# Attention stage of a two-block image kernel: scores, maxima and exponentials by pairs of head quads, values as 64-column halves, another order

## The chip, the cores and the metric

The kernel runs on one core of one Trainium2 chip. Its time is the device time of one execution in microseconds; lower is better. A core has five engines that each take their own instructions in order: PE (matrix products), DVE (vector), ACT (scalar, activations), POOL, and SP, which here issues the transfers. They wait for one another by semaphores.

## The reference, cut to what matters

The input `x` is (4, 128, 112, 112). Two blocks follow each other, each a residual on a group norm of its input. The change touches the first alone, attention in windows of 8x8 pixels with 8 heads of 16:

```
win = windows of gn(x), 64 tokens each           # 14 x 14 windows an image
xn  = layernorm(win) * ln_gamma + ln_beta
q, k, v = split(xn @ w_qkv.T + b_qkv)            # 8 heads, d = 16
scores  = einsum('nhqd,nhkd->nhqk', q * d**-0.5, k)
o   = einsum('nhqk,nhkd->nhqd', softmax(scores), v)
x   = x + (o @ w_out.T + b_out)                  # back from windows to image
x   = x + block_2(gn(x))                         # linear attention, 3x3 conv, MLP of 1024
```

## The kernel before, in words

Three stages follow each other: the window attention (lines 1367 to 1428 for PE), the contexts of the second block (`strip_c`), and its MLP (`step_d`). Only the first is changed.

An image has 14 strips of 8 rows, a strip 14 windows. A strip is worked on as two groups: `gg = 0` has 4 pairs of windows (512 tokens), `gg = 1` has 3 (384). `G` counts the groups over all images, 112 of them. `group_loop` (L306) calls each engine's `step(G, ...)` for each group; the strips in the middle of an image run in a hardware loop, the others are written out. Each `step` is a list in a fixed order, and each engine goes through its own: the order of the calls in the source is the order of the queue. A step mixes work on groups G-2 to G+3.

The work on a group, in the order of its data: ACT normalises the image strip into `xg` (`gn_apply`); PE transposes it to tokens in bank 5 (`ln_transpose`); DVE takes statistics (`ln_stats`, `ln_moments`), POOL the reciprocal root (`ln_rstd`), DVE writes `xc` (`ln_norm`); PE transposes back (`ln_back`), ACT writes `xn` and its high part (`xn_evac`), POOL its low part (`xn_low`). PE projects q (bank 7), k (bank 4) and v (bank 7): `project_q`, `project_k` by three split products each, `project_v` by one matmul for each pair of windows. ACT writes `qs` and two masked copies of k (`kx`), POOL casts both to bf16 (`q16`, `k16`), DVE copies v into `vx` in four pieces (`v_evac`, `value_blocks`).

The 8 heads lie as four quads `j` of 32 rows (two heads each). `score_rows` writes bf16 scores of quad j, queries in rows, to bank j; DVE takes their row maxima (`maxima`); PE transposes these (`transpose_maxima`, to bank 6) and DVE copies them (`mt_evac`). `score_cols` writes into the same banks j minus the maximum (L1334) and adds the fp32 scores with keys in rows (L1339); ACT takes exponentials into the one buffer `prob` (`exps`), and PE must not write the next score rows before (`prob_ready`). `attend` multiplies `prob` with `vx`, whose ones columns give the sums, half `h = 1` of a group (its last windows) into bank 7, half 0 into bank 6; DVE divides (`normalise`). `out_transpose` and `out_project` (bank 4), `ot_evac`, `ob_evac`, and POOL's `residual` add it to the image. DVE also takes the statistics for the group norms: of the next image (`next_stats`) and of the finished strip (`strip_stats`).

PE's `step` is, in order: score_rows(G), out_transpose(G-2), attend(G-1, 1), ln_transpose(G+2), out_project(G-2), attend(G-1, 0), transpose_maxima(G), project_q and project_k(G+1), score_cols(G), project_v(G+1), ln_back(G+2). DVE's: maxima(G), normalise(G-1, 1), ln_stats(G+2), mt_evac(G), ln_moments(G+2), normalise(G-1, 0), strip_stats (gg = 1), ln_norm(G+2), v_evac(G+1), next_stats (gg = 0).

Of the kernel before, what the change touches and what calls it, by code (L numbers as in the profile page):

```python
# [30 lines left out]
P = 128  # L31
# [46 lines left out]
def build(nc, x_d, vec_d, fc1b_d, dw_d, wm_d, cm_d, w1_d, w2_d, sel_d, out_d):  # L78
    with ExitStack() as ctx:
# [25 lines left out]
        qb = sb("qb", [P, NIMG])  # L105
        pws = [sb(f"pw_{n}", [P, 2, P], F32R) for n in ("hi", "lo")]
# [52 lines left out]
        prob = sb("prob", [P, QUADS, 8, 64], F32, stack_b)  # L159
# [12 lines left out]
        tstl = sb("tstl", [P, 2, STRIP], F32R, stack_b)  # L172
        kv = sb("kv", [P, 2, 4, 2, 2, P], F32, stack_b)
# [64 lines left out]
        smax_mm = sem("smax_mm")  # L238
# [3 lines left out]
        st_mm = sem("st_mm")  # L242
        prob_ready = sem("prob_ready")
# [135 lines left out]
        def value_blocks(gg):  # L379


            n = GROUP_PAIRS[gg]
            for w2 in range(2):
                for s in range(2):
                    src = bank[7][64 * w2:64 * w2 + 64, 0:P * n]\
                        .rearrange("p (t j s d) -> p t j s d", j=QUADS, s=2, d=HD)[:, :, :, s, :]
                    yield vx[64 * s:64 * s + 64, gg, w2:2 * n:2, :, (HD + 1) * s:(HD + 1) * s + HD], src
# [107 lines left out]
        def _(pool):  # L495
# [53 lines left out]
            def prologue():  # L549
                ln_rstd(0, 0)  # L550
                xn_low(0, 0)
                ln_rstd(1, 1)
                cast_q(0, 0)
                cast_k(0, 0)
# [7 lines left out]
            def step(G, i, s, gg, near):  # L562
                ng = 1 - gg
                if near(1):
                    xn_low(G + 1, ng)
                if near(-2):
                    residual(G - 2, strip_back(i, s)[1], gg)
                if near(2):
                    ln_rstd(G + 2, gg)
                if near(1):  # L570
                    cast_q(G + 1, ng)
                    cast_k(G + 1, ng)
                if at_norms(i, s) and gg == 0:
                    gn_coef(i + 1, norms_at(i))
# [45 lines left out]
        def _(act):  # L620
# [48 lines left out]
            def exps(G, gg):  # L669

                n = P * GROUP_PAIRS[gg]
                act.wait_ge(st_mm, G + 1)
                for j in range(QUADS):
                    m = a.activation(prob[:, j, 0:n // 64].rearrange("p w q -> p (w q)"), bank[j][:, 0:n], ACT.Exp)  # L674
                m.then_inc(prob_ready, 1)

            def ot_evac(G, gg):


                n = P * GROUP_PAIRS[gg]  # L680
                act.wait_ge(ot_mm, G + 1)
                a.activation(ot[:, gg, 0:n], bank[4][:, 0:n], ACT.Identity, bias=v("bv")).then_inc(ot_ready, 1)
# [7 lines left out]
            def prologue():  # L690
                act.wait_ge(gcoef_ready, 1)
                gn_apply(0, 0, 0, 0)
                gn_apply(1, 0, 0, 1)
                xn_evac(0, 0)
                gn_apply(2, 0, 1, 0)
                q_evac(0, 0)
                k_evac(0, 0)
                xn_evac(1, 1)

            def step(G, i, s, gg, near):  # L700
                ng = 1 - gg
                if near(-2):
                    ot_evac(G - 2, gg)
                    ob_evac(G - 2, gg)
                if near(3):
                    if at_norms(i, s) and gg == 1:
                        act.wait_ge(gcoef_ready, i + 2)
                    gn_apply(G + 3, *strip_after(i, s, 1 + gg), ng)
                if near(1):
                    q_evac(G + 1, ng)  # L710
                    k_evac(G + 1, ng)
                exps(G, gg)
# [115 lines left out]
        def _(dve):  # L828
# [45 lines left out]
            dve.wait_ge(weights_hi, 1)  # L874
            d.tensor_tensor(pws[1][:], wm[:, 0:2, :], pws[0][:].bitcast(F32), ALU.subtract).then_inc(weights_lo, 1)
# [87 lines left out]
            def maxima(G, gg):  # L963
                n = GROUP_PAIRS[gg]
                dve.wait_ge(smax_mm, G + 1)
                for j in range(QUADS):
                    m = d.tensor_reduce(mx[:, gg, 32 * j:32 * j + 2 * n],  # L967
                                        bank[j][:, 0:P * n].rearrange("p (e k) -> p e k", k=64), AX.X, ALU.max)
                m.then_inc(max_ready, 1)

            def mt_evac(G, gg):
                dve.wait_ge(mt_mm, G + 1)
                d.tensor_copy(mt16[:, gg, :], bank[6][:, 448:512].bitcast(BF16)).then_inc(mt_ready, 1)
# [49 lines left out]
            def prologue():  # L1023
                ln_stats(0, 0)
                ln_moments(0, 0)
                ln_norm(0, 0)
                ln_stats(1, 1)
                ln_moments(1, 1)
                ln_norm(1, 1)
                v_evac(0, 0)  # L1030

            def step(G, i, s, gg, near):
# [13 lines left out]
                mt_evac(G, gg)  # L1046
                if norms:
                    norm_variance(i + 1, norms_at(i), 6)
                if i + 1 < NIMG and isinstance(s, int) and s == 0:
                    next_stats(i, gg)  # L1050
                if near(2):
                    ln_moments(G + 2, gg)
                if near(-1):
                    normalise(G - 1, ng, 0)
                if gg == 1 and near(-2):
                    strip_stats(*strip_back(i, s), G - 1)
                if near(2):
                    ln_norm(G + 2, gg)
                if near(1):
                    v_evac(G + 1, ng)  # L1060
# [187 lines left out]
        def _(pe):  # L1248
# [50 lines left out]
            def project_v(G, gg):  # L1299
                for t in range(GROUP_PAIRS[gg]):  # L1300
                    c = slice(P * t, P * t + P)
                    m = mm(bank[7][:, c], xn[:, gg, c], wmat("wv"), start=True, stop=True)  # L1302
                m.then_inc(v_mm, 1)
# [5 lines left out]
            def score_rows(G, gg, reuse):  # L1309
# [4 lines left out]
                if reuse:  # L1314
                    pe.wait_ge(prob_ready, G)
                for w in range(2 * GROUP_PAIRS[gg]):
                    t, w2 = w // 2, w % 2
                    for j in range(QUADS):
                        m = mm(bank[j][64 * w2:64 * w2 + 64, P * t:P * t + P], q16[quad_rows(j), gg, w, :],  # L1319
                               k16[quad_rows(j), gg, w, :, :].rearrange("p s k -> p (s k)"), start=True, stop=True)  # L1320
                m.then_inc(smax_mm, 1)

            def transpose_maxima(G, gg):
                pe.wait_ge(max_ready, G + 1)
                tr(bank[6][:, 448:512].bitcast(BF16), mx[:, gg, :], ident16[:]).then_inc(mt_mm, 1)

            def score_cols(G, gg):
# [4 lines left out]
                for t in range(GROUP_PAIRS[gg]):  # L1332
                    for j in range(QUADS):
                        mm(bank[j][:, P * t:P * t + P], sel16[quad_rows(j), t, :], mt16[quad_rows(j), gg, :],  # L1334
                           start=(t == 0), stop=True, skip_group_check=True)
                for w in range(2 * GROUP_PAIRS[gg]):
                    for s in range(2):
                        for j in range(QUADS):
                            m = mm(bank[j][64 * s:64 * s + 64, 64 * w:64 * w + 64], kx[quad_rows(j), gg, w, s, :],  # L1339
                                   qs[quad_rows(j), gg, w, :], start=False, stop=True, skip_group_check=True)  # L1340
                m.then_inc(st_mm, 1)

            def attend(G, gg, h):


                for t in range(2 * h, min(2 * h + 2, GROUP_PAIRS[gg])):
                    for j in range(QUADS):
                        for q in range(4):
                            c, w = (t % 2) * QUADS * VCOLS + j * VCOLS, 2 * t + q // 2
                            m = mm(bank[6 + h][32 * q:32 * q + 32, c:c + VCOLS],  # L1350
                                   prob[:, j, w, 32 * (q % 2):32 * (q % 2) + 32], vx[:, gg, w, j, :],
# [3 lines left out]
            def out_transpose(G, gg):  # L1355
                pe.wait_ge(oh_ready[0], G + 1)
                pe.wait_ge(oh_ready[1], G + 1)
                for t in range(GROUP_PAIRS[gg]):
                    m = tr(bank[4][:, P * t:P * t + P], oh[:, gg, P * t:P * t + P], cmat("ident"))
# [7 lines left out]
            def prologue():  # L1367
# [4 lines left out]
                pe.wait_ge(xnl_ready, 1)  # L1372
                project_q(0, 0)
                project_k(0, 0)
                pe.wait_ge(q_ready, 1)
# [3 lines left out]
            def step(G, i, s, gg, near):  # L1379
                ng = 1 - gg  # L1380
                norms = at_norms(i, s) and gg == 0
                score_rows(G, gg, near(-1))
                if near(-2):
                    out_transpose(G - 2, gg)
                pe.wait_ge(v_ready, G + 1)
                if near(-1):
                    attend(G - 1, ng, 1)
                if near(2):
                    pe.wait_ge(xn_ready, G + 2)
                    ln_transpose(G + 2, gg)  # L1390
                if near(-2):
                    out_project(G - 2, gg)
                if near(-1):
# [4 lines left out]
                transpose_maxima(G, gg)  # L1398
                if near(1):
                    pe.wait_ge(xnl_ready, G + 2)  # L1400
                    if near(-1):
# [12 lines left out]
            def epilogue():  # L1414
                pe.wait_ge(ob_ready, NG - 2)
                out_transpose(NG - 2, 0)
                pe.wait_ge(prob_ready, NG)
                pe.wait_ge(v_ready, NG)
                attend(NG - 1, 1, 1)
                out_project(NG - 2, 0)  # L1420
                attend(NG - 1, 1, 0)
                pe.wait_ge(ob_ready, NG - 1)
                out_transpose(NG - 1, 1)
# [231 lines left out]
```

## Time and profile before

| | us |
|---|---|
| time, median of 3 runs (2667.43 to 2674.15) | 2669.88 |
| the profiled execution | 2671.07 |
| its span, first to last instruction | 2669.1 |
| busy PE | 2468.9 (92%) |
| busy DVE | 2159.1 (81%) |
| busy ACT | 2157.9 (81%) |
| busy POOL | 1716.4 (64%) |

The profile page gives these sums, the busy share of each engine over time, the chain of work that ended last, and the costliest groups of instructions. Rows of the trace name an instruction by its line in the kernel before. An engine can be said to wait for an instruction of another: "idle before, <-releaser". A matmul of fp32 operands appears as two instructions. Durations hold the time until the result is written, so the rows of an engine with a full queue overlap.

### The profile page before, as it was taken

What the parts mean: (1) busy time and instruction counts of PE and PEld (TensorE: products, weight loads), DVE (VectorE), ACT (ScalarE), POOL (GpSimd) and SP (SyncE); (2) the same over time, 40 slices, a digit from 0 to 9 for tenths busy, and PEclk for the clock granted to TensorE, in tenths of its full rate; (3) what the DMA queues carried; (4) which work ended last, traced back from release to release, by engine and by line L of the source; (5) the groups of instructions that cost most, each with busy time, mean ns of one, the idle gap of its engine ahead of it and who ended that gap; (6) DMA issues with size and microseconds to landing.
All of it is one profiled execution on the core that took longest, in us unless ns stands there. A gap on an engine that the chain in (4) does not pass through costs nothing.

```text
span 2669.1 us, 107195 instructions
## 1 busy us (share of the span) xinstructions
PE 2468.9 (92%) x43420; PEld 2088.9 (78%) x43420; DVE 2159.1 (81%) x4875; ACT 2157.9 (81%) x4093; POOL 1716.4 (64%) x1714
## 2 busy tenths in 40 slices
PE   3888789888888899899989999999999999999999
PEld 2666566666666667688978988898898899889888
DVE  6888788888988888667788888888888888888885
ACT  2777567766777777566779999999999999999998
POOL 2555445544555455366647777777777777777778
PEclk9999899999999999899989999999999999999999
DMA  4222122212221111144401101111110111100000
GB/s 151 70 76 72 51 82 76 75 59 78 78 74 53 48 55 49 50 136 127 138 15 42 41 32 42 42 42 38 42 42 32 42 41 42 39 28 21 17 21 25
DMA packets 55794, 152.18 MB, mean 57 GB/s; under 512 B 6608, under 2 KB 20944, under 8 KB 55632
## 3 DMA queue, kind: packets, MB, share of 16 engines
q1 hardware_dynamic: 55632, 149.93, 17.3%
q8 instruction: 113, 1.85, 0.3%
q14 instruction: 49, 0.40, 0.0%
HBM read 98.52 MB, written 51.38 MB: 56 GB/s over the span
## 4 chain that ended last, share of the span: by engine, by line
PE 72%; DVE 18%; issue 4%; ACT 2%; POOL 2%; DVEq 0%; SPq 0%; DMA 0%; POOLq 0%; ACTq 0%
PE bank L1285 17%; PE bank L1287 17%; PE bank L1286 17%; DVE mx L967 7%; PE bank L1440 6%; PE bank L1339 4%; DVE vx L960 3%; PE bank L1507 3%; PE bank L1302 2%; ACT prob L674 2%; DVE gst L835 2%; PE bank L1350 1%; DVE xc L953 1%; PE bank L1453 1%; POOL lnrs L526 1%
## 5 line engine op out<-in xcount | busy, mean ns | idle before, releaser
L613 POOL TENSOR_TENSOR hl<-hf,hh 128x448 fp32r<-128x448 f32 x896 | 1025.2, 1155 | 307.5 <-ACT hf L796 301.3
L795 ACT ACTIVATE hh<-bank,fc1i 128x448 fp32r<-128x448 f32 x896 | 584.9, 653 | 67.1 <-PE bank L1287 61.4
L1168 DVE SCALAR_TENSOR_TENSOR bank<-oring,dw,bank 128x448 f32<-128x448 f32 x896 | 614.9, 686 | 20.0
L796 ACT ACTIVATE hf<-bank,fc1i 128x448 f32<-128x448 f32 x896 | 586.2, 654 | 0.0
L1285 PE MATMUL bank<-t1h,w_hi 128*128 128x448 f32 x896 | 365.6, 408 | 5.9 <-DVE t1l L1187 5.6
L1285 PE MATMUL bank<-hh,w_hi 128*128 128x448 f32 x896 | 328.2, 366 | 0.0
L1287 PE MATMUL bank<-hl,w_hi 128*128 128x448 f32 x896 | 327.9, 366 | 0.0
L1287 PE MATMUL bank<-t1l,w_hi 128*128 128x448 f32 x896 | 327.4, 365 | 0.0
L1286 PE MATMUL bank<-hh,w_lo 128*128 128x448 f32 x896 | 327.2, 365 | 0.0
L1286 PE MATMUL bank<-t1h,w_lo 128*128 128x448 f32 x896 | 326.6, 365 | 0.0
L532 POOL TENSOR_TENSOR xn_lo<-xn,xn_hi 128x512 fp32r<-128x512 f32 x112 | 128.7, 1149 | 252.0 <-ACT xn_hi L651 252.0
L967 DVE TENSOR_REDUCE mx<-bank 128x8 bf16<-128x512 f32 x448 | 248.2, 616 | 11.1 <-PE bank L1319 8.2
L674 ACT ACTIVATE prob<-bank 128x512 f32<-128x512 f32 x448 | 207.4, 549 | 53.3 <-PE bank L1339 52.7
L560 POOL TENSOR_TENSOR ximg<-ximg,ob 128x512 f32 (+1 forms) x112 | 127.6, 1139 | 180.9 <-ACT ob L687 180.9
L960 DVE COPY vx<-bank 64x256 f32<-64x256 f32 x448 | 174.2, 389 | 62.5 <-PE bank L1302 57.9
L1350 PEld LDWEIGHTS bank<-vx,prob 128*32 128x32 f32 x12544 | 132.5, 110 | 110.2 <-issue 91.8
L1285 PEld LDWEIGHTS bank<-t1h,w_hi 128*128 128x128 f32 x896 | 168.7, 188 | 39.7 <-issue 26.7
L1286 PEld LDWEIGHTS bank<-t1h,w_lo 128*128 128x128 f32 x896 | 168.7, 188 | 32.3 <-issue 20.4
L1173 DVE TENSOR_TENSOR dwl<-bank,dwh 128x448 fp32r<-128x448 f32 x112 | 69.9, 624 | 144.2 <-ACT dwh L782 144.2
L953 DVE TENSOR_SCALAR xc<-bank,lnmv,lnrs 128x128 f32<-128x128 f32 x392 | 134.3, 402 | 58.6 <-POOL lnrs L526 58.6
L1287 PEld LDWEIGHTS bank<-hl,w_hi 128*128 128x128 f32 x896 | 168.3, 188 | 14.3
L687 ACT ACTIVATE ob<-bank,vec 128x512 f32<-128x512 f32 x112 | 71.0, 634 | 134.1 <-PE bank L1365 134.1
(167 smaller groups left out, 5966.4 us busy)
## 6 DMA issues: line engine op xcount, KB each, us to landing
ximg<-x SPq DMA_DIRECT2D x112, 448.0 KB, 3.4
ximg<-x_in SPq DMA_DIRECT2D x56, 448.0 KB, 3.4
x<-ximg SPq DMA_DIRECT2D x56, 448.0 KB, 2.5
y_out<-yb SPq DMA_DIRECT2D x112, 224.0 KB, 1.9
xs<-x_in SPq DMA_DIRECT2D x42, 448.0 KB, 3.4
wm<-wm_in SPq DMA_DIRECT2D x1, 512.0 KB, 5.3
w1f<-w_in SPq DMA_DIRECT2D x1, 512.0 KB, 8.8
w<-w_in SPq DMA_DIRECT2D x1, 512.0 KB, 9.6
```

What stands on the lines that cost most here:

```text
L613: g.tensor_tensor(hl[:, k, :], hf[:, k, :], hh[:, k, :].bitcast(F32), ALU.subtract).then_inc(hl_ready, 1)
L674: m = a.activation(prob[:, j, 0:n // 64].rearrange("p w q -> p (w q)"), bank[j][:, 0:n], ACT.Exp)
L795: a.activation(hh[:, j, :], p, ACT.Gelu, bias=bias)
L796: a.activation(hf[:, j, :], p, ACT.Gelu, bias=bias).then_inc(hf_ready, 1)
L953: m = d.tensor_scalar(xc[:, gg, P * t:P * t + P], bank[5][:, P * t:P * t + P], lnmv[:, gg, t, 0:1], lnrs[:, gg, t:t + 1], ALU.subtract, AL ...
L960: m = d.tensor_copy(dst, src)
L967: m = d.tensor_reduce(mx[:, gg, 32 * j:32 * j + 2 * n], bank[j][:, 0:P * n].rearrange("p (e k) -> p e k", k=64), AX.X, ALU.max)
L1168: m = d.scalar_tensor_tensor(acc, src, dw[:, k:k + 1], acc, ALU.mult, ALU.add)
L1285: mm(out, w[0], x[0], start=start, stop=False)
L1286: mm(out, w[1], x[0], start=False, stop=False)
L1287: return mm(out, w[0], x[1], start=False, stop=stop)
L1440: m = mm(bank[2 + cc][:, 2 * P * t:2 * P * t + 2 * P], x[:, sp, c], w.rearrange("p a b -> p (a b)"), start=(k == 0), stop=(k == 2))
```

## The change

- Scores, maxima and exponentials are done by pairs of quads: half `h` is quads 2h and 2h+1, with semaphores of its own (`smax_mm`, `st_mm`, `prob_ready`). `prob` has two buffers, by `gg`.
- `project_v` makes, for each window, two matmuls of 64 columns, for the first and the second head of all quads (`wvs` holds the weights so sorted), into the lower and upper 64 partitions of bank 4. `v_evac` copies each half by one instruction of 64 partitions, two for four.
- Banks: v goes from 7 to 4, the transposed maxima from 6 to 7, `out_transpose` from 4 to 6.
- Orders of all four engines' steps change. On PE `transpose_maxima` stands before `attend(G-1, 0)`, `project_k` comes before and `project_q` between the two halves of `score_cols` (half 1 first). On DVE both `normalise` follow `ln_moments`, then come the first half of `v_evac(G+1)`, `ln_norm`, `strip_stats` and the second half of `v_evac`.

```
+            for w in range(2 * GROUP_PAIRS[gg]):
+                for e in range(2):
+                    m = mm(bank[4][64 * e:64 * e + 64, 64 * w:64 * w + 64], xn[:, gg, 64 * w:64 * w + 64],
+                           wvs[:, e, :], start=True, stop=True)
             m.then_inc(v_mm, 1)
...
-            def v_evac(G, gg):
+            def v_evac(G, gg, e):
+                n = GROUP_PAIRS[gg]
                 dve.wait_ge(v_mm, G + 1)
-                for dst, src in value_blocks(gg):
-                    m = d.tensor_copy(dst, src)
-                m.then_inc(v_ready, 1)
+                src = bank[4][64 * e:64 * e + 64, 0:P * n].rearrange("p (w j d) -> p w j d", j=QUADS, d=HD)
+                d.tensor_copy(vx[64 * e:64 * e + 64, gg, 0:2 * n, :, (HD + 1) * e:(HD + 1) * e + HD], src)\
+                    .then_inc(v_ready, 1)
...
DVE step:
-                maxima(G, gg)
-                if near(-1):
-                    normalise(G - 1, ng, 1)
+                for h in range(2):
+                    maxima(G, gg, h)
                 if near(2):
                     ln_stats(G + 2, gg)
+                mt_evac(G, gg)
...
                 if near(2):
                     ln_moments(G + 2, gg)
...
                 if near(-1):
+                    normalise(G - 1, ng, 1)
                     normalise(G - 1, ng, 0)
+                if near(1):
+                    v_evac(G + 1, ng, 0)
+                if near(2):
+                    ln_norm(G + 2, gg)
                 if gg == 1 and near(-2):
                     strip_stats(*strip_back(i, s), G - 1)
-                if near(2):
-                    ln_norm(G + 2, gg)
                 if near(1):
-                    v_evac(G + 1, ng)
+                    v_evac(G + 1, ng, 1)
...
PE step:
-                score_rows(G, gg, near(-1))
+                if gg == 0:
+                    score_rows(G, gg, 0, near(-1))
                 if near(-2):
                     out_transpose(G - 2, gg)
-                pe.wait_ge(v_ready, G + 1)
+                if gg == 1:
+                    score_rows(G, gg, 0, near(-1))
+                score_rows(G, gg, 1, near(-1))
                 if near(-1):
                     attend(G - 1, ng, 1)
                 if near(2):
                     pe.wait_ge(xn_ready, G + 2)
                     ln_transpose(G + 2, gg)
+                pe.wait_ge(v_ready, G * 2 + 2)
                 if near(-2):
                     out_project(G - 2, gg)
+                transpose_maxima(G, gg)
                 if near(-1):
                     attend(G - 1, ng, 0)
...
-                transpose_maxima(G, gg)
                 if near(1):
                     pe.wait_ge(xnl_ready, G + 2)
+                    if near(-2):
+                        pe.wait_ge(ob_ready, G - 1)
+                    project_k(G + 1, ng)
+                score_cols(G, gg, 1)
+                if near(1):
                     if near(-1):
                         pe.wait_ge(oh_ready[1], G)
                     project_q(G + 1, ng)
-                    if near(-2):
-                        pe.wait_ge(ob_ready, G - 1)
-                    project_k(G + 1, ng)
-                score_cols(G, gg)
+                score_cols(G, gg, 0)
                 if near(1):
-                    pe.wait_ge(q_ready, G + 2)
+                    pe.wait_ge(k_ready, G + 2)
                     project_v(G + 1, ng)
                 if near(2):
                     ln_back(G + 2, gg)
```

On ACT the step becomes ot_evac, gn_apply, ob_evac, k_evac, exps half 1, q_evac, exps half 0, xn_evac (before: ot_evac, ob_evac, gn_apply, q_evac, k_evac, exps, xn_evac). On POOL `ln_rstd` goes ahead of `residual` and `cast_k` ahead of `cast_q`.

## Rows read from the trace of the kernel before

**Rows 1.** The page, chain that ended last, share of the span by engine.

```profile
PE 72%; DVE 18%; issue 4%; ACT 2%; POOL 2%; DVEq 0%; SPq 0%; DMA 0%; POOLq 0%; ACTq 0%
```

**Rows 2.** Windows, one strip: busy PE, PEld, DVE, ACT, POOL (instructions), clock, DMA, GB/s.

```profile
658.40:676.88 18.48, 16.53 (x585) 12.47 (x585) 16.56 (x51) 13.78 (x25) 9.81 (x13) 1.00 0.22 74
```

**Rows 3.** Waits from 300 to 1100 us: total us, times, longest.

```profile
PE bank L1319 <- ACT prob L674: 42.2, 82, 1.0
...
DVE vx L960 <- PE bank L1302: 41.1, 51, 2.6
```

**Rows 4.** Timeline of DVE: start, us, engine, line, op, xcount [idle before].

```profile
658.40 2.48 DVE L967 TENSOR_REDUCE mx<-bank 128x8 bf16<-128x512 f32 x4
660.80 0.20 DVE L980 RECIPROCAL rden<-bank 128x8 f32<-128x8 f32 x1
...
664.23 1.37 DVE L953 TENSOR_SCALAR xc<-bank,lnmv,lnrs 128x128 f32<-128x128 f32 x4 [0.98 <-POOL lnrs L526]
665.51 1.46 DVE L960 COPY vx<-bank 64x192 f32<-64x192 f32 x4
667.00 1.15 DVE L835 BATCH_NORM_STATS2 gst<-xs 128x448 f32 x2
668.19 1.95 DVE L967 TENSOR_REDUCE mx<-bank 128x6 bf16<-128x384 f32 x4
...
675.12 1.73 DVE L960 COPY vx<-bank 64x256 f32<-64x256 f32 x4 [0.57 <-PE bank L1302]
676.88 2.49 DVE L967 TENSOR_REDUCE mx<-bank 128x8 bf16<-128x512 f32 x4
```

**Rows 5.** Timeline of DVE in the last image, two strips' first maxima.

```profile
995.45 2.48 DVE L967 TENSOR_REDUCE mx<-bank 128x8 bf16<-128x512 f32 x4
...
1013.21 2.48 DVE L967 TENSOR_REDUCE mx<-bank 128x8 bf16<-128x512 f32 x4
```

**Rows 6.** Timelines of PE, and of ACT for the exponentials, in the same strip.

```profile
660.26 0.77 PE L1350 MATMUL bank<-vx,prob 128*32 128x34 f32 x64
660.96 0.23 PE L1325 MATMUL bank<-ident,mx 128*128 128x128 bf16 x1
...
662.68 0.40 PE L1334 MATMUL bank<-mt,sel 32*128 32x128 bf16 x16
663.01 1.59 PE L1339 MATMUL bank<-qs,kx 32*64 32x64 f32 x128
664.53 0.94 PE L1302 MATMUL bank<-wm,xn 128*128 128x128 f32 x6
665.65 0.65 PE L1280 MATMUL bank<-cm,xc 128*128 128x128 f32 x4 [0.18 <-DVE xc L953]
...
672.46 0.35 PE L1334 MATMUL bank<-mt,sel 32*128 32x128 bf16 x12
...
673.92 1.16 PE L1302 MATMUL bank<-wm,xn 128*128 128x128 f32 x8
...
664.64 2.06 ACT L674 ACTIVATE prob<-bank 128x512 f32<-128x512 f32 x4 [0.62 <-PE bank L1339]
```

**Rows 7.** The chain of waits from 658 to 677 us: start, us, what.

```profile
672.08 0.23 PE bank L1286
```

**Rows 8.** PE's timeline at idle stretches, and windows: granted clock third from last.

```profile
600.68 0.23 PE L1325 MATMUL bank<-ident,mx 128*128 128x128 bf16 x1 [2.14 <-DVE mx L967]
...
830.67 0.59 PE L1268 MATMUL bank<-gdev,cm 128*128 128x2 f32 x2 [3.00 <-DVE gdev L925]
...
871.24 0.23 PE L1325 MATMUL bank<-ident,mx 128*128 128x128 bf16 x1 [1.58 <-DVE mx L967]
...
1123.76 1.11 PE L1359 MATMUL bank<-cm,oh 128*128 128x128 f32 x4
...
828.40:835.10 6.70, 4.43 (x104) 3.80 (x109) 4.62 (x22) 1.81 (x3) 2.40 (x5) 0.59 0.01 2
```

More of the change, by code:

```diff
@@ L105, in build @@
         qb = sb("qb", [P, NIMG])
+        wvs = sb("wvs", [P, 2, P // 2])
         pws = [sb(f"pw_{n}", [P, 2, P], F32R) for n in ("hi", "lo")]
@@ L172, in build @@
         tstl = sb("tstl", [P, 2, STRIP], F32R, stack_b)
+        stack_p = ExitStack()
+        prob = sb("prob", [P, 2, QUADS, 8, 64], F32, stack_p)
+        stack_p.close()
         kv = sb("kv", [P, 2, 4, 2, 2, P], F32, stack_b)
@@ L237, in build @@
         k16_ready = sem("k16_ready")
-        smax_mm = sem("smax_mm")
+        smax_mm = [sem(f"smax_mm{n}") for n in range(2)]
         max_ready = sem("max_ready")
@@ L241, in build @@
         mt_ready = sem("mt_ready")
-        st_mm = sem("st_mm")
-        prob_ready = sem("prob_ready")
+        st_mm = [sem(f"st_mm{n}") for n in range(2)]
+        prob_ready = [sem(f"prob_ready{n}") for n in range(2)]
         pv_mm = sem("pv_mm")
@@ L377, in ring_copies, with quad_pair @@
                    ([(0, BLOCK_ROWS - 1)] if u == 3 and after else [])
[L379 to L387, printed above, removed]
+        def quad_pair(h):
+            return range(2 * h, 2 * h + 2)
         def hold(eng):
@@ L667, in k_evac, with exps @@
                              scale=v("mask_hi")).then_inc(k_ready, 1)
-            def exps(G, gg):
+            def exps(G, gg, h):
                 n = P * GROUP_PAIRS[gg]
[L672 to L675, printed above, removed]
+                act.wait_ge(st_mm[h], G + 1)
+                for j in quad_pair(h):
+                    m = a.activation(prob[:, gg, j, 0:n // 64].rearrange("p w q -> p (w q)"), bank[j][:, 0:n], ACT.Exp)
+                m.then_inc(prob_ready[h], 1)
             def ot_evac(G, gg):
@@ L874, in _ @@
             dve.wait_ge(weights_hi, 1)
+            d.tensor_copy(wvs[:].rearrange("p e (j d) -> p e j d", j=QUADS),
+                          wmat("wv").rearrange("p (j e d) -> p e j d", j=QUADS, e=2))
             d.tensor_tensor(pws[1][:], wm[:, 0:2, :], pws[0][:].bitcast(F32), ALU.subtract).then_inc(weights_lo, 1)
@@ L955, in ln_norm, with maxima @@
                 m.then_inc(xc_ready, 1)
-            def v_evac(G, gg):
+            def v_evac(G, gg, e):
+                n = GROUP_PAIRS[gg]
                 dve.wait_ge(v_mm, G + 1)
-                for dst, src in value_blocks(gg):
-                    m = d.tensor_copy(dst, src)
-                m.then_inc(v_ready, 1)
-            def maxima(G, gg):
+                src = bank[4][64 * e:64 * e + 64, 0:P * n].rearrange("p (w j d) -> p w j d", j=QUADS, d=HD)
+                d.tensor_copy(vx[64 * e:64 * e + 64, gg, 0:2 * n, :, (HD + 1) * e:(HD + 1) * e + HD], src)\
+                    .then_inc(v_ready, 1)
+            def maxima(G, gg, h):
                 n = GROUP_PAIRS[gg]
-                dve.wait_ge(smax_mm, G + 1)
-                for j in range(QUADS):
+                dve.wait_ge(smax_mm[h], G + 1)
+                for j in quad_pair(h):
                     m = d.tensor_reduce(mx[:, gg, 32 * j:32 * j + 2 * n],
@@ L1029, in prologue @@
                 ln_norm(1, 1)
-                v_evac(0, 0)
+                v_evac(0, 0, 0)
+                v_evac(0, 0, 1)
             def step(G, i, s, gg, near):
@@ L1337, in score_cols @@
                     for s in range(2):
-                        for j in range(QUADS):
+                        for j in quad_pair(h):
                             m = mm(bank[j][64 * s:64 * s + 64, 64 * w:64 * w + 64], kx[quad_rows(j), gg, w, s, :],
                                    qs[quad_rows(j), gg, w, :], start=False, stop=True, skip_group_check=True)
-                m.then_inc(st_mm, 1)
+                m.then_inc(st_mm[h], 1)
             def attend(G, gg, h):
@@ L1372, in prologue @@
                 pe.wait_ge(xnl_ready, 1)
+                project_k(0, 0)
                 project_q(0, 0)
-                project_k(0, 0)
-                pe.wait_ge(q_ready, 1)
+                pe.wait_ge(k_ready, 1)
                 project_v(0, 0)
@@ L1414, in epilogue @@
             def epilogue():
-                pe.wait_ge(ob_ready, NG - 2)
                 out_transpose(NG - 2, 0)
-                pe.wait_ge(prob_ready, NG)
-                pe.wait_ge(v_ready, NG)
+                for h in range(2):
+                    pe.wait_ge(prob_ready[h], NG)
+                pe.wait_ge(v_ready, NG * 2)
                 attend(NG - 1, 1, 1)
```

54 lines of the change are left out of this document (26 added, 28 removed).

## The prediction

> **What bounds the kernel now.** I read the page's share of the chain first, then the windows, then the waits, then one undisturbed strip engine by engine. The chain over the whole run is PE for 72% [rows 1], but most of that is the last stage, which the change leaves alone. The attention stage is the stretch from 48 to about 1128 us, 56 strips of two groups (4 and 3 window pairs). There no engine is at its limit: in one strip PE is busy 16.53 of 18.48 us and DVE 16.56 [rows 2]. The waits of the stage show who ends them: DVE for the value projection 51 times, by 41 us in all, PE for the exponentials 82 times, by half a microsecond each [rows 3]; both are short. The DVE rows of a strip are nearly without a hole: 0.98 us before `xc`, 0.57 us before `vx`, and the next strip begins 18.48 us after the last [rows 4]. So the stage is DVE's queue, with a little of PE's in it. A loop through both engines runs close under it: maxima end, PE projects, computes the score columns and the values, DVE copies the values, maxima begin again. In the strip of rows 4 it ended the wait for `vx` by 0.57 us. The last image has no statistics of a next image, and its strip takes 17.76 us [rows 5].
>
> I take occupancies from start to next start, since queued instructions overlap in the rows.
>
> **What changes on DVE.** The value copy becomes 2 instructions of 64x512 (or 384) for 4 of 64x256 (192). 4 of 256 take 1.76 us (675.12 to 676.88), 4 of 192 1.49 us (665.51 to 667.00) [rows 4]: 0.44 and 0.37 each, so 1.06 ns per column and 0.17 us fixed; 512 columns make 0.70 us and 384 0.57. That is 2.54 us a strip for 3.25: 0.7 us of DVE work goes. From below, at the rate of the maxima of the same width (0.60 and 0.47), it is 2.14. If DVE stayed the bound this would be the gain. Two probability buffers and halves with their own semaphores also let score rows of one pair of quads begin before the other pair's exponentials are done. But PE waits only that 0.5 us a group for the exponentials [rows 3], and DVE's order, not these waits, decides when maxima start. I count it nothing; it is worth at most 0.5 a group.
>
> **The new order makes the loop longer on both engines.** All engines take their instructions in order, so I walk the loop once per group, from M (maxima done) to P (`project_v` done) on PE and from P to the next M on DVE.
>
> From M to P, for both groups of a strip:
> - The maxima transpose and its handover, 0.2 each: 0.40. It starts about 0.1 us after the maxima end [rows 4, 6].
> - `attend(G-1, 0)`, which now stands behind the transpose that waits for the maxima, where before it ran beside them: 64 instructions in 0.70 us (660.26 to 660.96) [rows 6], twice 0.70: 1.40. This was hidden and is now on the path.
> - `project_k` and `project_q`, 3 matmuls each of 0.23 for 512 columns [rows 7] and three quarters of it for 384: 0.70 + 0.52 for each of the two: 2.44, as before.
> - The score columns. Now they take 1.85 (662.68 to 664.53) and 1.46 (672.46 to 673.92): 3.31 [rows 6]. In halves, two quads' row groups are at work instead of four. L1334 takes 0.33 for 16 and 0.28 for 12, 0.055 a round of four over a fixed 0.1; a half still needs a round per pair of windows, so it costs what the whole does: up to 0.61 more. L1339 runs at 11.9 ns over eight tiles (1.52 us for 128). One stream of 64 columns is half of the 0.11 us of a 128-column transpose, so with four tiles no better than 13.8 ns: 0.4 more, and a new start in each half. From below nothing is lost; from above each L1339 takes the 20.6 ns that L1334 has with four tiles, 2.5 us more in all. I take 0.9, nearest to the rounds: 4.21.
> - `project_v`: in place of 4 matmuls of 128 columns (0.99 us) and 3 (0.77) come 16 and 12 of 64 columns, each two instructions, 32 and 24, in two column tiles of the array. If the two overlap, 0.0275 each (1.54 us together), if they don't, 0.055 (3.1). Rows with four column tiles and all 128 rows (L1350) run at 11 ns for 34 columns, so they overlap, not fully: I take 0.0345, 1.93.
> - The handover to DVE, 0.2 each: 0.40.
>
> The sum is 10.8 us a strip. DVE has, after M, only the layer-norm statistics, the maxima copy, moments and both normalisations. The same instructions stand between the maxima and the wait for the roots now, from 660.80 to 663.25 (664.23 less 0.98) [rows 4]: 2.5 us a group. Then `v_evac(G+1, 0)` heads its queue and waits for P, about 5.4 us after M. That is the new stall, 2.5 to 3 us a group.
>
> From P to M on DVE, both groups:
> - both value copies of each group, 2.54.
> - `ln_norm`, now behind the first of them: 1.28 (664.23 to 665.51) for four, three quarters of it and a little for three, 1.00: 2.28. It used to run while PE was still at the score columns.
> - `strip_stats` in the one group (now behind the copy too) and `next_stats` in the other (as before), 667.00 to 668.19 less a wait's turn, 1.13 each: 2.26.
> - the maxima, 2.40 (658.40 to 660.80) + 1.87: 4.27.
>
> Sum 11.35. The other queues are not late: on ACT the last two exponentials start with the end of the columns and take 1.0 us (four take 2.06 [rows 6]), so they are done about when P is and before `ln_back`; the k copies run beside the first half of the columns; POOL is busy 9.81 of 18.48 us [rows 2], and `mt_ready` comes at M + 1.1 us, before PE reaches the first half at M + 1.5. SP's transfers keep their places by strip and get more time. `ln_norm` late means `ln_back` late, and PE's score rows are queued behind `ln_back`; they begin about P + 2.7, and the maxima could start at P + 3, but DVE is busy until P + 3.5. So that adds no more.
>
> A strip takes 10.8 + 11.35 = 22.1 us against 18.48, in the last image 22.1 - 1.2 = 20.9 against 17.76. 42 x 3.65 + 14 x 3.2 = 198 us. The same walk with the old order gives 18.2 for 18.48, so the walk is good to some tenths.
>
> Strips near an image's end are longer now: 42 x 18.48 + 14 x 17.76 = 1025 of the stage's 1080 us, so some 50 us are theirs, from the group-norm chain and from issue gaps. Their chains go through the same queues; I keep them. The weight copy `wvs` is one instruction, and the stages after this are unchanged.
>
> **The clock.** PE now idles from P until `ln_back`: 0.2 + 0.7 + 1.2, some 2.0 us as the profile counts idle time (a matmul's end comes 0.2 after the next could start), in every group. In the loop of before, each PE hole of over 2 us came with a fall of the granted clock to the lower level, 1.2 GHz: 3.00 us idle at 830.67, with 0.59 granted on average in the stretch around it, and 2.14 us at 600.68; one of 1.58 us at 871.24 did not [rows 8]. 2.0 lies between. At half clock four transposes take 1.11 us for 0.65 [rows 6, 8], and streams take twice as long; a fall costs about 0.9 us where it meets the path. I count one in four groups: 28 x 0.9 = 25 us. From above it is all 112, 100 us and more; from below nothing.
>
> The profiled run took 2671.07 us, 1.2 above the median of the runs. 2671 + 198 + 25 = 2894, less 1: 2893.
>
> **A rule on the weights.** The Trainium skill (TensorE: Matmul & The Clock Gate, section on packing small matmuls) says that a weight load overlaps running matmuls only when its row group differs; in `project_v` all loads use all rows. L1350 uses all rows too, in four column tiles, and goes at 11 ns a piece [rows 6], so this trace speaks against it. By the row the sum stays; by the rule it is that of the first rival.
>
> **Rivals.**
> - *Value projection serial.* Load and stream of each piece one after the other, 0.11 us (the pace of one 128-column piece, 0.99 for 8 less the start): 56 x 0.11 = 6.2 for 1.93, 4.2 a strip on the path: 2893 + 56 x 4.2 = 3128. For: no row here has just two column tiles. Against: L1350. 3%.
> - *Clock low in most groups.* As above, 2671 + 198 + 100 = 2970. For: the gap recurs in each group, and what ends it are transposes, and small tiles. Against: the hole is just short of those that fell. 17%.
> - *Tiles overlap as before, copies short.* Columns keep 3.31, values 1.54, copies 2.14, no clock loss: the strip is 20.4, 42 x 1.9 + 14 x 1.45 = 100: 2770. 15%.
> - *Faster: DVE stays the bound.* If P came before DVE is through its second normalisation, the wait is gone and only the shorter copies count: 18.48 - 0.7 - at most 0.57 and 0.98 of waits, 16.2 to 17.8, so 2545 to 2632; I say 2630. It needs M to P under 2.6 us, where the matmuls from M to P, q and k and the columns alone, already take (2.44 + 3.31)/2 = 2.9 us a group. It would decide if attend were not behind the maxima and `project_v` stood ahead of the columns. 6%.
> - The forecast 58%; 1% for no change, where shorter copies and overlap just cancel.
>
> **Numbers.** Its own range is 2820 to 2960. With the bounds (strip 20.4 to some 24) and the clock the range is 2775 to 2990. Under 0.3% (8 us) no measurement of this kernel tells a change. Faster 6%, same 1%, slower 93%.
>
> **What would show it.** After: a DVE wait for PE's L1302 of 2.5 us or more before the first `vx` of each group; strips of about 22.1 us; `vx` copies of 0.70 and 0.57; a PE hole near 2 us before L1280 released by `xc`; `attend` between the maxima transpose and the k projection; L1339 in halves of 64 lasting about 0.9 us. Wrong, if the DVE wait before `vx` is under 1 us, if `vx` copies are far from 0.7, or if strips stay near 18.

## The result, and the profile after

| | before | after |
|---|---|---|
| time, median of 4 runs (us) | 2671.28 | 3046.03 |
| lowest and highest | 2667.43, 2674.15 | 3036.51, 3048.32 |
| ratio, 95% interval | | 1.140 [1.137, 1.143] |
| busy PE, DVE (us) | 2468.9, 2159.1 | 2743.4, 2123.6 |
| mean granted PE clock | 0.984 | 0.926 |

The kernel became slower by 375 us; I had said 222, with a range that ended at 2990. The direction and the place were right and the size was not.

The whole loss is in the attention stage. These rows are windows, of after and then of before: a stretch, then busy us of PE, PE's weight loads, DVE, ACT, POOL, the granted clock, the share of DMA and GB/s. The stage is the first row of each.

```profile
48.00:1520.00 1472.00, 1225.95 (x35105) 909.67 (x35093) 891.66 (x2641) 778.36 (x1356) 558.37 (x683) 0.86 0.15 48
1520.00:3046.00 1526.00, 1505.67 (x10592) 1359.08 (x10591) 1206.29 (x1929) 1376.83 (x2728) 1150.99 (x1014) 0.99 0.15 48
```

```profile
48.00:1128.00 1080.00, 939.79 (x32647) 711.47 (x32647) 921.28 (x2848) 765.93 (x1340) 545.80 (x675) 0.98 0.20 65
1128.00:2669.00 1541.00, 1518.45 (x10706) 1369.79 (x10705) 1211.37 (x1942) 1382.84 (x2740) 1160.36 (x1021) 0.99 0.15 47
```

DVE has 30 us less to do in the stage and is busy for 0.61 of it instead of 0.85. PE has the same products to make but is busy for 286 us more, at 0.86 of its clock instead of 0.98. The clock was at its lower level for 427 us of the stage in 80 spells (55 us before).

The waits of after, 300 to 1300 us (total us, times, longest), beside [rows 3]:

```profile
DVE vx L965 <- PE bank L1312: 333.7, 76, 8.2
...
PE bank L1288 <- DVE xc L955: 139.4, 76, 1.9
```

The wait for `vx` was 41 us in 800; it is 334 in 1000, 4.4 us each, in nearly every group. The second line was 5.4 us in 31 short waits before: now PE waits for `xc` in nearly every group, 1.8 us each, before `ln_back`.

DVE's timeline of one strip of after, beside [rows 4] (start, us, engine, line, operation, what it waited for):

```profile
701.70 0.68 DVE L965 COPY vx<-bank 64x512 f32<-64x512 f32 x1 [4.21 <-PE bank L1312]
702.31 1.03 DVE L955 TENSOR_SCALAR xc<-bank,lnmv,lnrs 128x128 f32<-128x128 f32 x3
703.27 1.13 DVE L835 BATCH_NORM_STATS2 gst<-ximg  x2
704.43 0.70 DVE L965 COPY vx<-bank 64x512 f32<-64x512 f32 x1
705.16 2.48 DVE L972 TENSOR_REDUCE mx<-bank 128x8 bf16<-128x512 f32 x4
...
714.64 0.55 DVE L965 COPY vx<-bank 64x384 f32<-64x384 f32 x1 [4.38 <-PE bank L1312]
...
718.79 1.95 DVE L972 TENSOR_REDUCE mx<-bank 128x6 bf16<-128x384 f32 x4 [0.55 <-PE bank L1330]
...
726.91 0.68 DVE L965 COPY vx<-bank 64x512 f32<-64x512 f32 x1 [3.88 <-PE bank L1312]
```

The strip takes 25.2 us (701.70 to 726.91); the strips inside the images take 24.5 to 26.5. No instruction of DVE got slower. It stands still 8.8 us of 25.2.

PE's timeline of the second group of that strip, beside [rows 6]:

```profile
720.80 0.23 PE L1336 MATMUL bank<-ident,mx 128*128 128x128 bf16 x1
720.96 0.77 PE L1361 MATMUL bank<-vx,prob 128*32 128x34 f32 x64
721.66 0.51 PE L1293 MATMUL bank<-xn_hi,pw_hi 128*128 128x512 f32 x1
...
722.57 0.34 PE L1345 MATMUL bank<-mt,sel 32*128 32x128 bf16 x6
722.84 0.93 PE L1350 MATMUL bank<-qs,kx 32*64 32x64 f32 x48
723.69 0.50 PE L1293 MATMUL bank<-xn_hi,pw_hi 128*128 128x512 f32 x1
...
724.59 0.34 PE L1345 MATMUL bank<-mt,sel 32*128 32x128 bf16 x6
724.86 0.93 PE L1350 MATMUL bank<-qs,kx 32*64 32x64 f32 x48
725.72 1.15 PE L1312 MATMUL bank<-wvs,xn 128*64 128x64 f32 x32
728.61 0.55 PE L1288 MATMUL bank<-cm,xc 128*128 128x128 f32 x3 [1.75 <-DVE xc L955]
```

From the maxima transpose to the copy of the values PE goes without a pause: attend 0.70, k 0.91, columns 1.12, q 0.90, columns 1.13, values 1.19 with the handover. Then comes the hole of 1.75 us. In the first group each half of the columns takes 1.42, and k and q take 0.72 each (start to start of these rows, cut):

```profile
709.40 0.44 PE L1293 MATMUL bank<-xn_hi,pw_hi 128*128 128x384 f32 x1
...
710.12 0.40 PE L1345 MATMUL bank<-mt,sel 32*128 32x128 bf16 x8
...
711.54 0.44 PE L1293 MATMUL bank<-xn_hi,pw_hi 128*128 128x384 f32 x1
...
712.26 0.40 PE L1345 MATMUL bank<-mt,sel 32*128 32x128 bf16 x8
```

`out_project` of that group, behind the hole, took 1.92 us. The last row is the kernel before, at the full clock, 1.02:

```profile
706.49 1.92 PE L1376 MATMUL bank<-ot,wm 128*128 128x512 f32 x2
708.20 0.31 PE L1336 MATMUL bank<-ident,mx 128*128 128x128 bf16 x1
...
659.31 1.02 PE L1365 MATMUL bank<-ot,wm 128*128 128x512 f32 x2
```

The maxima had ended at 707.64, so here PE came 0.56 us late to their transpose, by the low clock.

### The profile page after: what moved, and what is told of

It reads as the page before. It is cut to its first block, busy times and chain, and to the rows that moved or that the text cites. A ratio compares the mean times of both kernels' runs of the same rounds, so it can differ in the third digit from the quotient of the medians.

```text
span 3046.4 us, 111988 instructions
## 1 busy us (share of the span) xinstructions
PE 2743.4 (90%) x45772; PEld 2277.0 (75%) x45772; DVE 2123.6 (70%) x4652; ACT 2162.8 (71%) x4093; POOL 1719.0 (56%) x1714
## 4 chain that ended last, share of the span: by engine, by line
PE 85%; DVE 11%; issue 2%; DVEq 1%; ACT 1%; DMA 0%; SPq 0%; POOL 0%; ACTq 0%; POOLq 0%
PE bank L1293 17%; PE bank L1295 15%; PE bank L1294 15%; PE bank L1350 8%; PE bank L1457 5%; PE bank L1361 5%; DVE xc L955 4%; PE bank L1312 4%; PE bank L1376 3%; PE bank L1524 3%; DVE mx L972 3%; PE bank L1345 2%; PE bank L1282 2%; PE bank L1288 2%; DVE gst L835 1%
## 5 line engine op out<-in xcount | busy, mean ns | idle before, releaser
L965 DVE COPY vx<-bank 64x512 f32<-64x512 f32 x224 | 139.4, 622 | 489.5 <-PE bank L1312 486.0
L646 ACT ACTIVATE xn<-bank,vec 128x512 f32<-128x512 f32 x112 | 81.1, 724 | 286.6 <-PE bank L1288 286.6
L671 ACT ACTIVATE prob<-bank 128x512 f32<-128x512 f32 x448 | 219.2, 543 | 86.5 <-PE bank L1350 86.5
L1288 PE MATMUL bank<-cm,xc 128*128 128x128 f32 x392 | 77.7, 322 | 206.2 <-DVE xc L955 206.2
L1350 PE MATMUL bank<-qs,kx 32*64 32x64 f32 x12544 | 245.9, 227 | 0.0
L1350 PEld LDWEIGHTS bank<-qs,kx 32*64 32x64 f32 x12544 | 214.2, 139 | 24.7 <-issue 2.9
L1288 PEld LDWEIGHTS bank<-cm,xc 128*128 128x128 f32 x392 | 47.1, 157 | 222.2 <-DVE xc L955 222.1
L1361 PEld LDWEIGHTS bank<-vx,prob 128*32 128x32 f32 x12544 | 156.5, 129 | 62.3 <-issue 53.4
L661 ACT ACTIVATE kx<-bank,par,vec 128x512 f32<-128x512 f32 x112 | 81.2, 725 | 165.0 <-PE bank L1295 165.0
```

The source lines that it names most:

```text
L671: m = a.activation(prob[:, gg, j, 0:n // 64].rearrange("p w q -> p (w q)"), bank[j][:, 0:n], ACT.Exp)
L1288: m = tr(bank[5][:, P * t:P * t + P], xc[:, gg, P * t:P * t + P], cmat("ident"))
L1361: m = mm(bank[6 + h][32 * q:32 * q + 32, c:c + VCOLS], prob[:, gg, j, w, 32 * (q % 2):32 * (q % 2) + 32], vx[:, gg, w, j, :], start=True, ...
```

## The experiments

Times are medians of 4 runs; each ratio is to the kernel before in the same batch (2670 to 2672 us). The changed kernel's is 1.140 [1.137, 1.143]. "Less" means less than its 3046.0 us, measured in another batch. A steady strip is one in the middle of an image.

### ln_norm ahead of the first value copy

```
-                if near(1):
-                    v_evac(G + 1, ng, 0)
                 if near(2):
                     ln_norm(G + 2, gg)
+                if near(1):
+                    v_evac(G + 1, ng, 0)
```

> The changed kernel with ln_norm ahead of the first half of v_evac in DVE's order, as it was before. Theory 'loop': ln_norm (2.3 us a strip) leaves the stretch from project_v to the next maxima and runs in DVE's wait of 4 us, and PE's hole before ln_back shrinks from 1.9 us to under 0.5, so the clock stays up too: 130 us for the first and some 80 for the second, about 2835. Without the clock's part about 2915. Rival 'the wait only moves' (DVE's wait for project_v grows by as much): 3040.

Measured: 2857.8 us, ratio 1.071 [1.069, 1.073]: 188 us less than the changed kernel, the largest single part, and near the 210 of the loop with its clock; the rival of a wait that only moves is refuted. The strip is 21.6 us. DVE's timeline:

```profile
706.98 1.05 DVE L955 TENSOR_SCALAR xc<-bank,lnmv,lnrs 128x128 f32<-128x128 f32 x3 [0.21 <-POOL lnrs L523]
709.95 0.68 DVE L965 COPY vx<-bank 64x512 f32<-64x512 f32 x1 [1.92 <-PE bank L1312]
```

`xc` now runs inside the wait for `vx`, which falls from 4 to 1.9 us, and `ln_back` follows `project_v` without a hole. The clock of the whole run goes from 0.926 to 0.968. PE still has a hole in each strip, of 1.39 us before the maxima transpose, 44 of them in the stage, but the clock is at its lower level in 12 spells and not in 80.

### The score columns in one piece

```
-                score_cols(G, gg, 1)
+                score_cols_whole(G, gg)       # all four quads in turn
                 if near(1):
                     ...
                     project_q(G + 1, ng)
-                score_cols(G, gg, 0)
```

> The changed kernel with score_cols in one piece over all four quads again (L1345 and L1350 of the changed kernel, four row groups at a time), ahead of project_q; all else as changed. Theory 'tiles': the halves run at 14.6 ns a piece plus a start each, the whole at 12 ns, so a strip loses 1.8 us of columns and some of a restart of the projection: 56 x 2 = 110 us less, about 2935. Theory 'instruction supply': the pieces are bound by their issue, the whole is no faster when attend, k and the columns stand in one run: under 30 us less, 3020 or more.

Measured: 2929.9 us, ratio 1.098 [1.095, 1.100], 116 us less, as the first expectation had it. Two things changed at once: the halves became one piece, and q went behind all columns. PE in this kernel, against 1.09 us for each half of 64 (710.45 to 711.54 in the changed kernel):

```profile
702.12 0.40 PE L1342 MATMUL bank<-mt,sel 32*128 32x128 bf16 x16
702.45 1.59 PE L1348 MATMUL bank<-qs,kx 32*64 32x64 f32 x128
703.97 0.44 PE L1293 MATMUL bank<-xn_hi,pw_hi 128*128 128x384 f32 x1
```

128 pieces take 1.52 us, 11.9 ns each; 2 x 64 take 2.18, 17.0 ns each. With the rounds of maxima (L1342 here, L1345 in the changed kernel) the group's columns take 1.85 and not 2.84 us. The granted clock rose too (0.946 for the profiled run, from 0.926), so a part of the 116 is the clock's.

### The columns in two passes, in the order of before

The same question without the changed order: quads 0 and 1, then 2 and 3, nothing else.

```
+                for h in range(2):
                     for t in range(GROUP_PAIRS[gg]):
-                        for j in range(QUADS):
+                        for j in range(2 * h, 2 * h + 2):
```

> The kernel before with score_cols in two passes, quads 0 and 1, then 2 and 3, nothing else changed (one semaphore, same place). Theory 'tiles': two passes of 1.42 and two of 1.12 us for 3.31 us a strip, 1.8 us more, of which DVE's holes and the loop's slack of some 0.6 hide a part: 56 x 1.0 to 1.8, 2730 to 2770. Rival 'the slowness of the halves in the changed kernel comes from their place between projections': within 15 us of 2671.

Measured: 2775.4 us, ratio 1.039 [1.038, 1.041]: 106 us more than before. That is 5 us over the expected range: the strip grows from 18.49 to 20.25 us, by the 1.8 of the columns, and nothing of it was hidden. PE's timeline:

```profile
667.94 0.34 PE L1335 MATMUL bank<-mt,sel 32*128 32x128 bf16 x6
668.21 0.93 PE L1340 MATMUL bank<-qs,kx 32*64 32x64 f32 x48
669.07 0.34 PE L1335 MATMUL bank<-mt,sel 32*128 32x128 bf16 x6
669.34 0.93 PE L1340 MATMUL bank<-qs,kx 32*64 32x64 f32 x48
670.20 1.16 PE L1302 MATMUL bank<-wm,xn 128*128 128x128 f32 x8
```

2.26 us for what took 1.46 in [rows 6], and as much as in the changed kernel (1.12 + 1.13): the place of the halves between the projections is not the cause.

### The hole filled

```
                     project_v(G + 1, ng)
+                pe.wait_ge(prob_ready[1], G + 1)
+                for _ in range(14):
+                    mm(bank[3][:, 0:2 * P], pws[0][:, 0, :], pws[0][...], start=True, stop=True)
```

> The changed kernel with 14 more matmuls of 256 columns (about 1.6 us at full clock) behind project_v, written to bank 3, which nobody reads any more at that point; they fill the hole in which PE waits for xc. Theory 'clock': the hole brings the low clock in most groups (427 us of the stage in the changed kernel), and about half of its cost lies on the path; the granted clock of the stage goes from 0.86 to over 0.95 and the time falls from 3046 to about 2930, although PE has more work. Theory 'loop only': the low clock mostly meets matmuls off the path; the time stays within 20 us of 3046, or is longer by what the filler delays.

Measured: 2982.2 us, ratio 1.116 [1.114, 1.118]: 64 us less, with more work. It is between the two expectations: the clock counts, with little over half of what I had put on it (64 of 116 us). The stage's granted clock is 0.96 (third from the end):

```profile
48.00:1460.00 1412.00, 1325.92 (x36791) 1032.47 (x36792) 891.41 (x2646) 778.67 (x1362) 560.17 (x686) 0.96 0.15 50
```

Its steady strip takes 23.85 us, against 25.1 on average for the steady strips of the changed kernel: 1.25 us a strip is the clock's. `ln_back` starts 1.70 and 1.88 us after the first value copy of the two groups in both kernels, so the extra matmuls delay nothing. The columns take in it what they took above at the full clock, so 23.85 is what the order alone costs. It also gives a cleaner price for `ln_norm`: from 23.85 to the 21.62 of the kernel with `ln_norm` ahead is 2.23 us a strip, where the forecast had 2.28.

### attend ahead of the maxima transpose

```
-                transpose_maxima(G, gg)
                 if near(-1):
                     attend(G - 1, ng, 0)
+                transpose_maxima(G, gg)
```

> The changed kernel with attend(G-1, 0) ahead of transpose_maxima again. Theory 'all of it is on the path', as my forecast had it: 0.7 us a group goes, 112 x 0.7 = 78 us, about 2968. Theory 'PE has no slack there': in the changed kernel's trace PE reaches transpose_maxima only when the maxima are done (0.1 us after in one group, 0.6 us after in the other, out_project at half clock before it), so attend moves from behind M to before it and pushes the transpose back by the same; under 0.4 us in one of two groups is won: 3020 to 3046.

Measured: 2991.2 us, ratio 1.121 [1.119, 1.123]: 55 us less. Neither expectation holds. It is more than the slack that I read, and less than the 78 us of a full 0.7 us a group. From the end of the maxima to the first value copy, on average over 27 steady strips, the groups of four pairs went from 6.67 to 5.95 us and those of three only from 6.83 to 6.71. How that splits between slack and clock (0.944 for the run, from 0.926) was not told apart.

### Three parts undone together

> The changed kernel with three parts undone together: ln_norm ahead of the first value copy, columns in one piece, attend ahead of the maxima transpose. Theory 'the parts add up' (the loop, the tiles and the clock that falls in the hole): 3046 - 188 - 116 - 20 = 2722, with the low clock gone nearly 2700. Rival 'another engine takes over': not under 2780.

Measured: 2686.8 us, ratio 1.0067 [1.005, 1.008]: 359 us less, and 13 under the 2700 expected. The clock of the stage is 0.98 again. The three parts alone gave 188 + 116 + 55, also 359, but that they agree to the microsecond is luck: each of them also brought back some of the clock (427 us at the lower level fell to 147, 287 and 304, and in this kernel to 44), so that gain is counted more than once, and attend alone gave less than its 78. The sum to trust is that of the strips at nearly full clock: 23.85, less 2.23 for `ln_norm`, 5.08 - 3.31 for the columns and 1.40 for attend, is 18.45; measured 18.50. DVE's waits in a strip of 18.50 us are those of a queue that is nearly full:

```profile
659.26 1.05 DVE L955 TENSOR_SCALAR xc<-bank,lnmv,lnrs 128x128 f32<-128x128 f32 x3 [0.21 <-POOL lnrs L523]
661.45 0.68 DVE L965 COPY vx<-bank 64x512 f32<-64x512 f32 x1 [1.14 <-PE bank L1312]
```

What is left of the change (two probability buffers, maxima and exponentials by halves, the banks, the other orders, the value halves) costs 17 us against before. The value halves alone gain 30 (below), so the rest costs some 45: its strip is 18.50 us where theirs is 17.82, and 17.45 in the last image. Which part does it was not tested. The rows point to `strip_stats`, 1.1 us, which stood ahead of the value copies before and now stands behind the first.

### q directly behind k

```
                     project_k(G + 1, ng)
+                    ...
+                    pe.wait_ge(mt_ready, G + 1)
+                    project_q(G + 1, ng)
                 score_cols(G, gg, 1)
-                if near(1): ... project_q(G + 1, ng)
                 score_cols(G, gg, 0)
```

> The changed kernel with project_q directly behind project_k (and the copy of q on ACT behind that of k), both halves of the columns behind them. Theory 'starts cost': a run of large matmuls between small tiles costs about 0.2 us at its start, which the forecast left out; two of four starts a strip go, 0.4 us, with what follows for the columns' starts 20 to 35 us, about 3018. Rival 'starts cost nothing': within 8 us of 3046.

Measured: 3040.0 us, ratio 1.138 [1.136, 1.140], 6 us less; the intervals overlap. The expectation of 3018 failed, and the time is inside the rival's 8 us. The trace says more than the time. In the one group the two projections take 1.55 us (714.67 to 716.22) for 1.81 apart, so a start is worth 0.26. In the other q now waits, for the first normalisation or for the copy of the maxima (a wait that this edit put ahead of q), and the two take 1.60 (702.10 to 703.70) for 1.44. What the starts give, a wait takes back; which of the two waits it is was not told apart.

### The value halves alone, in the order of before

```
+                for w in range(2 * GROUP_PAIRS[gg]):
+                    for e in range(2):
+                        m = mm(bank[7][64 * e:64 * e + 64, 64 * w:64 * w + 64], xn[...], wvs[:, e, :], ...)
...
+                for e in range(2):
+                    m = d.tensor_copy(vx[64 * e:64 * e + 64, ...], bank[7][64 * e:64 * e + 64, ...])
```

> The kernel before with the values as 64-column halves alone (wvs, two column tiles in project_v into bank 7, two copies of 64 partitions for four), its order and banks unchanged. Theory 'DVE is the bound there': 0.7 us of DVE work less a strip, less what project_v costs more (0.15): 2671 - 30 to 40 = 2635. Rival 'two column tiles are slow': project_v at 0.055 a piece adds 1.3 us a strip in front of the copies, 2671 + 30 = 2700.

Measured: 2641.3 us, ratio 0.989 [0.987, 0.991]. This part of the change is a gain. The strip goes from 18.49 to 17.82 us, which is the 0.7 us that DVE has less to do. PE, then DVE:

```profile
657.62 1.15 PE L1307 MATMUL bank<-wvs,xn 128*64 128x64 f32 x32
658.70 0.55 PE L1285 MATMUL bank<-cm,xc 128*128 128x128 f32 x3
```

```profile
658.82 1.39 DVE L965 COPY vx<-bank 64x512 f32<-64x512 f32 x2 [0.67 <-PE bank L1307]
660.25 2.48 DVE L972 TENSOR_REDUCE mx<-bank 128x8 bf16<-128x512 f32 x4
```

32 pieces in 1.08 us, against 0.99 for the 8 of before, which move half as many columns in all (32 x 64 against 8 x 128): two column tiles overlap.

### A version that beats both

The value halves, and `next_stats` of the group gg = 0 moved ahead of `ln_norm`, into DVE's wait of 0.98 us for the roots [rows 4].

> The kernel before with the values as 64-column halves (2641 us) and next_stats of gg = 0 ahead of ln_norm instead of behind v_evac, into DVE's wait of 0.98 us for lnrs. Theory 'DVE's queue sets the strip': 0.5 to 0.9 us less in the 33 strips in the loops of three images, 2611 to 2625. Rival 'the loop through PE sets it now': within 8 us of 2641.

Measured: 2627.7 us, ratio 0.985 [0.983, 0.986]: 13.6 us less than the value halves alone, 1.5% less than before. The gain is 3 us short of the expected range; the strip goes from 17.82 to 17.44.

With k ahead of q as well:

> The kernel before with values as 64-column halves and next_stats ahead of ln_norm (2628 us), and with k ahead of q on PE, ACT and POOL: project_k need not wait for the first normalisation. Theory 'the loop through PE now sets the strip' (17.44 us): 0.2 us a group of wait goes, up to 20 us, 2605 to 2620. Rival 'DVE's queue still sets it': within 8 us of 2628.

Measured: 2628.4 us, ratio 0.983 [0.981, 0.985]. No difference from 2627.7. The expectation counted on a wait that was already gone: from 300 to 1000 us the projections wait for a normalisation 28 times, 5.9 us in all, in the kernel of the value halves, 6 times, 1.6 us in all, with `next_stats` moved, and never here. What sets the strip of 17.4 to 17.5 us stays open.

## Why the prediction was right, and where it was wrong

**The loop** was right. The new wait is DVE's for `project_v`, in nearly every group, and the parts that I put on the path (`ln_norm` behind the first copy, attend behind the maxima, the columns in halves) were found there: the first and the last alone, attend in full only together with them. `ln_norm` I put at 2.28 us a strip, 128 us in all; the strips show 2.23, and undoing it gave 188 us, with what the clock gives back when the hole closes.

**The copies and the values** were right: 0.70 and 0.57 us a copy forecast, 0.72 and 0.58 measured, start to start, where two follow each other in the kernel of the value halves (658.82 to 660.25 for the wide pair); 1.10 us for the 32 pieces of `project_v` forecast (at 0.0345), 1.08 measured. The rival of a serial value projection is refuted by the 32 pieces in 1.08 us. It was also what the rule on weight loads would give in the Trainium skill (TensorE: Matmul & The Clock Gate, section on packing small matmuls); the measurement goes against that rule for two column tiles.

**The step that failed is the sum from M to P on PE, 10.8 us a strip.** In the kernel with the filled hole, at nearly full clock, the steady strips have 12.33 there, and 11.53 from P to M for 11.35. Two terms of the sum were too small:
- *The score columns*, taken at 4.21 us between 3.31 and 5.8. They take 2 x 1.42 + 2 x 1.12 = 5.08. I put the doubled L1334 rounds (0.61) and the slower L1339 (0.4) into the bounds, and then took 0.9, under what they make together. The rounds came as said, 0.6 more. L1339 in halves took 1.2 us a strip more, not 0.3 to 0.4: each half also starts anew. 0.87 us a strip, 49 us.
- *The projections*, taken at 2.44 us "as before". I multiplied a matmul's pace and left out its start: k and q take 0.72 each in the one group (709.40 to 710.12, 711.54 to 712.26) and 0.91 and 0.90 in the other: 3.25. 0.8 us a strip, 45 us. "As before" was wrong too. Before, the two together take 1.22 us in the one group (661.46 to 662.68 in [rows 6]) and 1.55 in the other (670.91 to 672.46), 2.77 and not 2.44; the walk with the old order, 18.2 for 18.48, was short by this. So 0.33 was misread in the old kernel, and 0.48 is the second start in each group, which was put at nothing. Undoing these second starts gained 6 us and not 27, since a wait took their place.

The starts of before, of the same strip:

```profile
661.46 0.41 PE L1285 MATMUL bank<-xn_hi,pw_hi 128*128 128x384 f32 x1 [0.27 <-DVE oh L984]
...
670.91 0.47 PE L1285 MATMUL bank<-xn_hi,pw_hi 128*128 128x512 f32 x1 [0.48 <-DVE oh L984]
```

Together 22.1 + 0.87 + 0.8 = 23.8, and the steady strip of the kernel with the filled hole is 23.85. That it fits so closely is in part luck: the values with their handover came out 0.2 us under the forecast, and the way from P to M 0.2 over.

**The clock** was a rival at 17% (2970) and a term of 25 us in the forecast, a fall in one group of four. Its price was right and its count was not. It fell much oftener, 80 spells in 112 groups (11 in the stage of before), with holes of 1.75 and 1.93 us, where [rows 8] had left the stretch from 1.58 to 2.14 open. Filling the holes took away 70 spells and 64 us, 0.9 each, as forecast. In steady strips it is 1.25 us each, 70 us, 45 more than the forecast had.

49 + 45 + 45 = 139 of the 153 us that were missing. The last image adds some 13: I had its strip shorter by 1.2 us since `next_stats` is gone, but its steady strips are shorter by 0.25 on average (24.9 for 25.2; 23.60 for 23.86 with the hole filled), because PE's score rows, queued behind `ln_back`, then hold the maxima:

```profile
1317.37 1.95 DVE L972 TENSOR_REDUCE mx<-bank 128x6 bf16<-128x384 f32 x4 [0.96 <-PE bank L1330]
```

I had computed that rows would let the maxima start 0.5 us before DVE was ready, and not asked what happens when DVE has less to do. The faster rival is refuted: P came 6 to 7 us after M, not under 2.6.

The range failed because its upper end held a strip of 24 us with the clock's small share; with the clock's full price on it, it would have been 2671 + 56 x 5.5 + 70, some 3050.

## What to carry to other kernels

Walk the loop between two in-order engines by what stands in each queue between the two handovers, and add the start of every run of matmuls, not only their pace; an instruction that is free inside a wait can cost its full length once it stands behind it, as `ln_norm` did. Count the array tiles that a stretch of small matmuls keeps busy: here half the row groups made each piece slower (17.0 ns for 11.9, starts included) and the rounds of maxima had to be made twice. A new hole on PE can cost twice, by itself and by the clock of what follows, here 70 us. And a slow change can hold a good part: timed alone, the value halves gave 1.1%.

## What the runs showed of the hardware that I had not expected

- With eight tiles in turn, L1339 runs at 11.9 ns a piece over 128 pieces; with four tiles at 17.0 ns over 64, which includes the start. With four tiles the pieces of a round start 7 ns apart, and the next round 58 ns after the round before, a little over the 0.055 us that the prediction worked out for a stream; the second round of each half comes 106 ns after the first.
- PE holes of 1.75 and 1.93 us, one in each group, were enough to keep the mean granted clock of the stage at 0.86, with 427 us at the lower of its two levels (1.2 GHz). Before, a single hole of 1.58 us had not brought it down. With the holes filled it was 0.96. With `ln_norm` ahead, 44 holes of 1.39 us, one a strip, went with 12 spells at the lower level in the whole stage.
